# fp32 queries and keys in 32-row bands for the last attention, in place of three bf16 parts

## The reference

```python
q = (x @ Wq + bq).reshape(B, S, H, Dh)        # H = 16 heads of Dh = 16
k = (x @ Wk + bk).reshape(B, S, H, Dh)
v = (x @ Wv + bv).reshape(B, S, H, Dh)
scores = jnp.einsum('bqhd,bkhd->bhqk', q, k) / jnp.sqrt(jnp.float32(Dh))
attn = jax.nn.softmax(scores, axis=-1)
ctx = jnp.einsum('bhqk,bkhd->bqhd', attn, v).reshape(B, S, D)
```

## Time and profile before

| | us |
|---|---|
| runs (three) | 5720.04 to 5744.4, median 5739.33 |
| span of the profiled execution | 5746.7 |
| attention of the layer before (g) | 2251 to 3445 |
| projections and layernorm (p) | 3448 to 3987 |
| last attention (e) | 3993 to 4928 |
| last stage (m) | 4932 to 5744 |

### The profile page before, as it was taken

The page is one execution under the profiler, slowest core; times in us unless marked ns, Lnnn a source line. Parts: engine busy times, 40 slices in busy tenths (PEclk is TensorE's granted clock), DMA queues, the critical chain, the costliest instruction groups (busy, mean ns, idle before and its releaser), DMA issues. The chain is left out here.

```text
span 5746.7 us, 99792 instructions
## 1 busy us (share of the span) xinstructions
PE 4422.5 (77%) x26575; PEld 2884.0 (50%) x26575; DVE 3816.5 (66%) x9299; ACT 2478.7 (43%) x5698; POOL 596.5 (10%) x928
## 2 busy tenths in 40 slices
PE   6999788300388885878787776776999998689898
PEld 5777566200255553555555555554555554344444
DVE  4555333588687877777767764555777777477776
ACT  2222333565333333677777762222666666200000
POOL 0111000000000001000000001111111111122221
PEclk9999899655699997777777787887999999899998
DMA  2222233679644443222222225555333333211110
GB/s 81 74 75 68 105 140 139 196 240 396 229 132 124 132 124 91 62 71 71 71 71 71 71 52 144 156 156 139 85 91 92 92 90 88 63 46 47 49 47 25
DMA packets 380380, 617.00 MB, mean 107 GB/s; under 512 B 43575, under 2 KB 310389, under 8 KB 380277
## 3 DMA queue, kind: packets, MB, share of 16 engines
q1 hardware_dynamic: 367956, 614.35, 36.6%
q0 software_dynamic: 12320, 1.40, 0.2%
HBM read 345.02 MB, written 269.21 MB: 107 GB/s over the span
## 5 line engine op out<-in xcount | busy, mean ns | idle before, releaser
L1670 DVE TENSOR_REDUCE e_neg<-ps 91x1 f32<-91x273 f32 x1536 | 571.8, 427 | 139.2 <-PE ps L1491 131.8
L1603 ACT ACTIVATE e_probT<-ps 91x273 f32<-91x273 f32 x1536 | 491.6, 392 | 291.7 <-PE ps L1491 290.9
L1218 PE MATMUL ps<-k_downT,f_o 128*91 128x256 f32 x1152 | 259.7, 385 | 455.9 <-DVE f_o L1126 455.7
L2345 PE MATMUL ps<-m_we,m_xT 128*128 128x512 f32 x1104 | 530.8, 630 | 0.0
L1218 PEld LDWEIGHTS ps<-k_downT,f_o 128*91 128x91 f32 x1152 | 182.8, 161 | 524.5 <-issue 456.9
L1489 PE MATMUL ps<-c_mask_kq,c_identb 91*91 91x91 bf16 x1536 | 322.7, 241 | 105.9 <-ACT g_probT L1603 74.3
L1491 PE MATMUL ps<-e_k,e_q 96*91 96x273 bf16 x1536 | 344.3, 306 | 62.9 <-DMA e_k<-s_parts 28.1
L2279 DVE SCALAR_TENSOR_TENSOR m_acc<-ps,m_weight,m_acc 128x256 f32<-128x256 f32 x552 | 261.7, 481 | 185.7 <-PE ps L2345 175.9
L1491 PE MATMUL ps<-g_q,g_k 102*91 102x273 bf16 (+5 forms) x1536 | 328.5, 294 | 50.6 <-DVEq L1676 49.9
L2345 PEld LDWEIGHTS ps<-m_we,m_xT 128*128 128x128 f32 x1104 | 214.8, 202 | 227.9 <-issue 213.5
L1491 PE MATMUL ps<-e_q,e_k 128*91 128x273 bf16 x1536 | 285.7, 290 | 40.1 <-DMA e_q<-e_shift 38.2
(11 more groups left out here) (306 smaller groups left out, 9733.9 us busy)
## 6 DMA issues: line engine op xcount, KB each, us to landing
s_gate<-b_gu SPq DMA_DIRECT2D x32, 819.0 KB, 4.7
s_up<-b_gu SPq DMA_DIRECT2D x32, 819.0 KB, 6.1
c_g<-s_gate SPq DMA_DIRECT2D x32, 819.0 KB, 7.2
s_gated<-c_g SPq DMA_DIRECT2D x32, 819.0 KB, 8.6
d_g<-s_gated SPq DMA_DIRECT2D x32, 819.0 KB, 10.4
d_u<-s_up SPq DMA_DIRECT2D x32, 819.0 KB, 10.7
s_o<-d_o SPq DMA_DIRECT2D x32, 819.0 KB
f_o<-s_o SPq DMA_DIRECT2D x32, 819.0 KB, 4.8
```

Source lines behind the costliest of these rows:

```text
L1218: last = nc.tensor.matmul(ps[0:R, t // 2, (t % 2) * D:(t % 2 + 1) * D], o[:, u, k, t * R:(t + 1) * R], downT[:, k, :], start=(k == 0), sto ...
L1603: nc.scalar.activation(probT[0:R, p % 8, b, :], src, ACT.Exp, scale=float(HD) ** 0.5 if kinds[h] == COS else 1.0)\
L1670: last = nc.vector.tensor_reduce(neg[:, u, t, h:h + 1], src, AX.X, ALU.max, negate=True)
L2345: last = nc.tensor.matmul(ps[0:R, EBANK[m % 4], :], xT[:, u, k, t * R:(t + 1) * R], we[:, k, 2 * p:2 * p + 2, :].rearrange("p e d -> p (e ...
```

## The change

Three things change together.

1. **Layout.** Heads are put into four groups of four. A head has a band of 32 rows: 16 dimensions, one row for the shift, 15 empty ones. `phase_g1` gets its weights in this order from the host (`by_group`), so queries and keys are eight matmuls of 128 columns (group x query/key) in place of four. They leave PSUM as fp32, queries by ACT, keys by DVE, one operation each; the key's bias has a 1 in the shift row.
2. **Token tiles.** The attention takes tokens as 128, 128 and 17. For the 17 that are left, POOL lays the four heads of a group side by side, each in its own block of rows and zero elsewhere (`qrest`, `krest`), so that one matmul over all 128 rows serves four heads. Values of these 17 tokens lie in such blocks as well (`vrest`).
3. **A new function** `attention_full` takes the place of `attention_core` for the last attention. Look and main scores are fp32 matmuls over 16 and 17 rows of one band. PSUM has four banks for looks (two units of two), two for mains, one for the products, one for transposes. In PE's program a look in one band and a main in another (`ORDER` is 2, 3, 0, 1) alternate:

```diff
+            def look(n, u, g, a, t):
+                y = UNITS * g + a
+                if t == 0:
+                    pe.wait_ge(S["looked"].sem, S["looked"].at(n, y - 1))
+                rows = slice(32 * a, 32 * a + HD)
+                last = nc.tensor.matmul(ps[:, LOOK[y % 2][t], 0:T], qk[rows, u, g, Q, t * 128:(t + 1) * 128],
+                                        qk[rows, u, g, K, :], start=True, stop=True)
...
+            def look_rest(n, u, g):
...
+                pe.wait_ge(S["rest"].sem, S["rest"].at(n, 2 * g + 2))
+                pe.wait_ge(S["looked"].sem, S["looked"].at(n, y - 1))
+                nc.tensor.matmul(ps[:, LOOK[y % 2][0], 0:T], qrest[:, u, g].rearrange("p a t -> p (a t)"),
+                                 qk[:, u, g, K, :], start=True, stop=True).then_inc(S["look"].sem, 1)
...
+            def main(n, u, g, x, t):
+                z, a = TILES * g + 2 * x + t, ORDER[x]
+                pe.wait_ge(S["exp"].sem, S["exp"].at(n, z - 1))
+                rows = slice(32 * a, 32 * a + HD + 1)
+                nc.tensor.matmul(ps[:, MAIN[z % 2], 0:T], qk[rows, u, g, K, t * 128:(t + 1) * 128],
+                                 qk[rows, u, g, Q, :], start=True, stop=True).then_inc(S["s"].sem, 1)
...
+                for g in range(GROUPS):
+                    if g == 0 and mains:
+                        turn(now, u, 1)
+                    if g == 2 and pres:
+                        turn(then, tu, 0)
...
+                    for half in range(2):
+                        for a in (2 * half, 2 * half + 1):
+                            for t in range(2):
+                                if pres:
+                                    look(then, tu, g, a, t)
+                                if mains:
+                                    main(now, u, g, a, t)
+                        if half == 0:
+                            if g >= 2 and mains:
+                                turn_back(now, u, g - 2, (then, 1) if g == 2 and pres else None)
...
+                            if g >= 1 and mains:
+                                combine(now, u, mi, g - 1)
...
+                    if pres:
+                        look_rest(then, tu, g)
+                    if mains:
+                        main_rest(now, u, g)
```

`turn` transposes the maxima of two groups, ACT copies them out as fp32, and POOL's five DMAs lay them into the shift rows. `combine` makes the product with the values, 12 matmuls in four column bands, once a group. DVE takes one maximum over two banks (`largest`) and one over the rest (`largest_rest`):

```diff
+                nc.vector.tensor_reduce(neg[:, u, g // 2, 0:2, 2 * a + g % 2], ps[:, first:first + 2, 0:T], AX.X, ALU.max,
+                                        negate=True).then_inc(S["looked"].sem, 1)
```

In `phase_g1` the queries and keys:

```diff
-                for j in range(2 * CT):
+                for j in range(2 * GROUPS):
...
+                    emptied = S["k_out" if j % 2 else "q_out"]
+                    if j >= 4:
+                        pe.wait_ge(emptied.sem, emptied.at(n, (j - 4) // 2 + 1))
+                    elif j >= 2:
+                        pe.wait_ge(emptied.sem, emptied.at((n[0], n[1] - 1)))
                     for k in range(CT):
-                        last = nc.tensor.matmul(ps[:, QK_BANK[j], 0:T],
-                                                wqk[:, k, j // CT, (j % CT) * 128:(j % CT + 1) * 128],
-                                                xT[:, u, k, :], start=(k == 0), stop=(k == CT - 1))
+                        last = nc.tensor.matmul(ps[:, QK_BANK[j % 4], 0:T], wqk[:, k, j, :], xT[:, u, k, :],
+                                                start=(k == 0), stop=(k == CT - 1))
...
-            pipeline(dve, NB, ((values, 0), (residual, 1), (lower_parts_q, 0), (normalise, 1),
-                               (lower_parts_k, 0)))
+            pipeline(dve, NB, ((values, 0), (residual, 1), (keys_first, 0), (normalise, 1), (keys_second, 0)))
```

More of the change, by code:

```diff
@@ L886 @@
 RP = 128
+GROUPS = H // 4
+WHOLE = 256
+REST = T - WHOLE
+KEYS = (128, 128, REST)
 def pipeline(eng, NB, stages):
@@ L1771, in phase_g1 @@
         S = signals(ctx, nc, "p", cT=1, cT_out=1, y=1, hb=1, h3=1, bn=NT + 1, mv=1, eps=1, rstd=1, xn=NT, xT=1,
-                    xT_out=1, v=1, v_out=1, qk=2 * CT, hi=2 * CT, rest=2 * CT, mid=2 * CT, lo=2 * CT)
-        banks = [lambda k, u=u: ps[:, 4 * u + k, :] for u in range(2)]
+                    xT_out=1, v=1, v_out=1, qk=2 * GROUPS, q_out=GROUPS, k_out=GROUPS)
         QK_BANK = (4, 5, 2, 3)
-        WEIGHTS = 16 * (4 + 2 * CT + 2)
+        WEIGHTS = 16 * 6
         block = ctx.enter_context(nc.Block())
@@ L1816, in store_parts @@
             def store_parts(n, u, i):
-                for j in range(2 * CT):
-                    sp.wait_ge(S["lo"].sem, S["lo"].at(n, j + 1))
+                for half in range(2):
+                    sp.wait_ge(S["q_out"].sem, S["q_out"].at(n, 2 * half + 2))
                     sp.sem_inc(passed, 1)
-                    sp.dma_start(parts_dram[batch_of(n), j // CT, :, (j % CT) * 128:(j % CT + 1) * 128]
-                                 .rearrange("k r t -> r k t"), parts[:, u, j]).then_inc(p_stored[u], 16)
@@ L1823, in _ @@
[L1823 to L1824 removed]
+                    sp.wait_ge(S["k_out"].sem, S["k_out"].at(n, 2 * half + 2))
+                    sp.sem_inc(passed, 1)
+                    sp.dma_start(qk_dram[batch_of(n), :, half * GROUPS:(half + 1) * GROUPS],
+                                 qk[:, u, half * GROUPS:(half + 1) * GROUPS]).then_inc(p_stored[u], 16)
@@ L1825, in _ @@
+            sp.dma_start(wqk[:], wqk_dram.rearrange("(k p) (j n) -> p k j n", p=128, n=128)).then_inc(w_loaded, 16)
             sp.dma_start(proj[:], proj_dram.rearrange("(k p) n -> p k n", p=128)).then_inc(w_loaded, 16)
             sp.dma_start(wv[:], wv_dram.rearrange("(k p) n -> p k n", p=128)).then_inc(w_loaded, 16)
[L1827 to L1830, removed]
+            sp.dma_start(bqk[:], bqk_dram).then_inc(w_loaded, 16)
@@ L1837, in _ @@
             for u in range(2):
-                for s, times in ((h_stored, 1), (x_stored, 1), (p_stored, 2 * CT), (v_stored, 1)):
+                for s, times in ((h_stored, 1), (x_stored, 1), (p_stored, 2), (v_stored, 2)):
                     sp.wait_ge(s[u], 16 * times * (NB // 2))
@@ L1858, in _ @@
         def _(act):
-            for k in ("cT_out", "xT_out", "hi", "mid"):
+            for k in ("cT_out", "xT_out", "q_out"):
                 S[k].give(act)
@@ L1918, in values @@
                 dve.wait_ge(S["v"].sem, S["v"].at(n))
-                dve.wait_ge(v_stored[u], 16 * i)
-                bias = bv[:].rearrange("p (h w) -> p h w", w=HD)
+                dve.wait_ge(v_stored[u], 32 * i)
                 for t in range(NT):
-                    x = ps[0:R, 6 + t // 2, (t % 2) * D:(t % 2 + 1) * D].rearrange("p (h w) -> p h w", w=HD)
-                    last = nc.vector.tensor_tensor(vp[:, u, t, :, 0:HD], x, bias, ALU.add)
+                    rows = KEYS[t]
+                    x = ps[0:rows, 6 + t // 2, (t % 2) * D:(t % 2 + 1) * D].rearrange("p (h w) -> p h w", w=HD)
+                    last = nc.vector.tensor_tensor(vp[0:rows, u, t, :, 0:HD], x,
+                                                   bv[0:rows].rearrange("p (h w) -> p h w", w=HD), ALU.add)
@@ L1939, in lower_parts_q, with keys @@
[L1939 to L1948, removed]
-            pipeline(dve, NB, ((values, 0), (residual, 1), (lower_parts_q, 0), (normalise, 1),
-                               (lower_parts_k, 0)))
+            def keys(n, u, i, groups):
+                dve.wait_ge(p_stored[u], 32 * i)
+                for g in groups:
+                    dve.wait_ge(S["qk"].sem, S["qk"].at(n, 2 * g + 2))
+                    nc.vector.tensor_scalar(qk[:, u, 2 * g + 1], ps[:, QK_BANK[(2 * g + 1) % 4], 0:T],
+                                            bqk[:, 2 * g + 1:2 * g + 2], None, ALU.add).then_inc(S["k_out"].sem, 1)
@@ L1953, in _, with keys_first, keys_second @@
+            def keys_first(n, u, i):
+                keys(n, u, i, range(GROUPS // 2))
+            def keys_second(n, u, i):
+                keys(n, u, i, range(GROUPS // 2, GROUPS))
+            pipeline(dve, NB, ((values, 0), (residual, 1), (keys_first, 0), (normalise, 1), (keys_second, 0)))
         @block.tensor
@@ L1975, in values @@
                     for k in range(CT):
-                        last = nc.tensor.matmul(ps[0:R, 6 + t // 2, (t % 2) * D:(t % 2 + 1) * D],
-                                                xT[:, u, k, t * R:(t + 1) * R], wv[:, k, :],
+                        last = nc.tensor.matmul(ps[0:KEYS[t], 6 + t // 2, (t % 2) * D:(t % 2 + 1) * D],
+                                                xT[:, u, k, t * 128:t * 128 + KEYS[t]], wv[:, k, :],
                                                 start=(k == 0), stop=(k == CT - 1))
@@ L2384, in program @@
     extra1 = scratch("extra1", [NB, 2, SLOTS, NHYP, T], BF16)
-    parts2 = scratch("parts2", [NB, 2, PARTS, HD * H, T], BF16)
-    v1, v2 = (scratch(n, [NB, R, NT * H * VW]) for n in ("v1", "v2"))
+    qk2 = scratch("qk2", [NB, 128, 2 * GROUPS, T])
+    v1, v2 = scratch("v1", [NB, R, NT * H * VW]), scratch("v2", [NB, T, H * VW])
     ctx = ExitStack()
@@ L2456, in ffn, with by_group @@
     def ffn(*names):
```

(10 more changed lines are left out.)

380 lines of the change are left out of this document (335 added, 45 removed).

## The result

The changed kernel took **6033.69 us** (median of four runs, 6017.9 to 6046.95) beside 5741.86 before: a ratio of 1.0503, interval 1.0476 to 1.0530. It is slower, as forecast, but by 5.0% where 1.1% was forecast, and outside the range. The profiled execution has a span of 6022.9 us for 5746.7, 276 us more.

A forecast was written before the change was run, and what follows sets the result against it. TensorE's program order was taken to bind, waiting for maxima, exponentials and shift rows. Attention +131, its start -7, stage before -62 and tail +1 gave +63 us: 5802 us, 1.1% slower, range 5685 to 5930.

The forecast's parts named there:

- its start: Start of the last attention: less to set up by memsets before TensorE's first load, -7 us, bounds -9 and 0.
- stage before: Stage before the last attention: TensorE without its pause and at full clock, 14.1 us a batch for 16.11, -62 us.
- the group's sum of 7.60 us: Last attention, four heads: two halves, value product between, 17-token matmuls behind; with waits 32.1 us a batch, +131 us.
- the rival of a lower clock: Last attention: matmuls of 16 or 17 rows bring the clock to 0.81, +198 us, 6000 us in all; chance 0.09.
- The round: Main scores' two banks: wake, load, two passes, drain, consumer's wake and exponential take 1.21 us for two matmuls.
- a half: Half a group of the attention, four mains: 1.21 us and two matmuls in one band, 0.92, make 2.13 us.
- the middle: Between a group's two halves: mode changes, load, three transposes and the product with the values, 2.13 us.
- the rests: Behind a group's second half: two full-array matmuls of the 17 tokens with load and mode changes, 1.21 us.
- the wait behind the turn: In one of two groups of the attention, the turn of the maxima waits for the last maximum, 0.64 us more.
- Strict order among row bands: Attention: each half waits one pass more, 1.8 us a batch, +59 us, 5861 us in all; chance 0.06.
- bands in series: Attention: row bands run one after another, 13.3 us a batch, +425 us, 6227 us in all; chance 0.09.
- faster loop: Attention: loads and mode changes hide under the other band's stream, 5682 us, or 5742 if half hidden; chance 0.28.

The follow-up runs named there:

- Experiment 1: The changed kernel with look and main scores over all 32 rows of a band, the added rows holding zeros: 5871.5 us, 1.0229 against the kernel before.
- Experiment 5: The changed kernel with 32 rows for looks and mains, and three single PSUM banks for each in place of four and two: 5748.98 us, 1.0004.
- experiment 3: The changed kernel with each main in the same band as the look beside it (ORDER 0, 1, 2, 3): 6926.94 us, 1.2057.
- Experiment 4: The kernel before, with query and key matmuls of the stage before the last attention made twice, filling TensorE's pause: 5719.99 us, 0.9961.
- experiment 7: The changed kernel, still 16 and 17 rows, with three single banks each for looks and mains, and 17-token matmuls and maxima turn in mid-group: 5731.39 us, 0.9940.

## Why the prediction was wrong

The account from span to span, 276 us (predicted +63):

| step | predicted | measured |
|---|---|---|
| attention, between batches, at full clock | +131 | 31 x (32.8 - 27.95) = +150 |
| its first and last batch (what remains of the stage) | 0 | +39 |
| its clock | 0 (rival: +198) | 31 x (37.97 - 32.8) = +160 |
| its start | -7 | -12.5 |
| stage before | -62 | -53 |
| other stages, the unevenness of before, and rounding | +1 | -8 |

- **The step that failed** is the group's sum of 7.60 us, with "a batch 32.1 us", taken at full clock for the whole stage. It has no term for the clock; the runs show 5.2 us a batch, 160 us in all. The prediction had the mechanism, as the rival of a lower clock (0.09): "Matmuls now fill 16 or 17 rows of a band". Its 6000 us, at a clock of 0.81 and 38.3 us a batch, is close to what happened: 0.82, 37.97 us, 6034. In part that is luck: its clock term is 198 us for 160, and the 39 us of the first and last batch are not in it. The prediction gives no reason for the 0.09 but the two clocks of before, 0.96 and 0.81; where it argues a clock, for the stage before, it goes by the pause alone ("without the pause and so at full clock"). Experiment 1 shows that the clock was the missing term: the zero rows alone give back 162 us between the medians.
- **The full-clock sum was nearly right.** Two groups take 16.39 us (7.90 + 8.49) for 16.04. The round is 1.22 for 1.21; a half is 2.36 to 2.42 for 2.13, since after the round the loads are exposed for the second main too (4432.81, behind an exponential); the middle is 1.99 for 2.13, the rests 1.12 for 1.21, and the wait behind the turn 0.64 as predicted. Experiment 5 confirms the round through two banks as a cause, worth 0.9 us a group.
- **First and last batch** were not counted: looks run a whole batch ahead and mains end alone. From the first look to the first exponential it is now 33.3 us for 17.5, and from the last maximum to the last exponential 43.9 for 16.9, both in stretches of low clock (0.50 and 0.65; the last stretch before had 1.00).
- **Strict order among row bands** is refuted by the common start at 4431.10 and the look that overtakes at 4431.12, **bands in series** by the first of these and by experiment 3. The **faster loop** (loads and changes hidden) did not occur: the load that waits for an exponential is in the trace at 4432.32.
- **The stage before** went as worked out: no pause, a clock of 0.97, 14.45 us for 14.1. Queries and keys are 7.37 for 7.36; the values are 2.89 for 2.6, of which about 0.09 each is lost at the step onto the weights of 17 columns and at the step off them (0.31 from pass to pass for 0.215). Experiment 4 puts the clock at half of its gain or more (0.90 of 1.66 us a batch).
- **The start** gained more than its bound of 9: TensorE's first look comes 12.9 us after the stage before ends, 25.4 before, and 2.4 of that is the gap between the stages.

## What to carry to other kernels

When a change swaps matmuls over 96 and 128 rows for ones over 16 and 17, price the stage at both clocks: a TensorE that is busy all the time is not thereby at full clock, and padding a band with zero rows can be a cheap cure (162 us here). Conversely, a pause that looks free may cost the clock of what follows it. Before giving a ring of banks one round per matmul, count the round: wake, load, passes, drain and consumer are a chain, and rings of three single banks took 0.9 us off each group here.

## What was not expected of the hardware

- The granted clock was 0.82 with TensorE busy 98% of the stage and 0.55 with it busy 99%; 15 or 16 rows more in each matmul, with nothing in them to add, brought 0.82 to 0.95, at no cost in the matmul's own time (2.36 us a half either way).
- Matmuls added to a pause made a stage 26 us shorter (512.3 for 538.6).
- At equal rows the clock was 0.82 with the two-bank loop and 0.92 with the loop of experiment 7. Rows in one loop (experiment 1) and the loop at the same rows (experiment 7) both move the clock; what exactly the chip counts stays open.
- A look in one row band started 0.54 us ahead of a look and a main that stand before it in the program (4431.12 for 4431.66).
